# Scan layer with its front and tail in another order, the gate on the Vector engine, a semaphore per first weight and three unread products

## What is computed

```
x = x + 0.5 * _L0_ffn_ref(_layernorm(x), ...)     # mixture of experts
x = x + _L0_attn_ref(_layernorm(x), ...)          # windowed attention
x = x + 0.5 * _L0_ffn_ref(_layernorm(x), ...)     # mixture of experts
x = x + 0.5 * _L1_ffn_ref(_layernorm(x), ...)     # ternary feed-forward
x = x + _L1_attn_ref(_layernorm(x), ...)          # scan layer
x = x + 0.5 * _L1_ffn_ref(_layernorm(x), ...)     # ternary feed-forward
```

```
delta = softplus(delta @ dt_proj_w.T + dt_proj_b)
h = exp(delta * a) * h + delta * b * u            # per token, channel and state
y = sum over the states of h * c
y = (y + u * D_param) * silu(res)
return y @ out_proj_w.T + out_proj_b
```

## Time and profile before

| | us |
|---|---|
| median of 3 runs | 563.32 |
| lowest and highest of them | 561.24, 566.46 |
| profiled execution, its own time | 567.4 |
| its span, first to last instruction | 565.7 |

### The profile page before, as it was taken

How to read it: one execution, slowest core, us unless ns; L and a number is a source line. 1 busy time by engine, 2 the same in 40 slices (tenths; PEclk the granted TensorE clock), 3 DMA queues, 4 the chain that set the end, 5 groups by cost and what they waited for, 6 DMA issues and landing times.

```text
span 565.7 us, 10087 instructions
## 1 busy us (share of the span) xinstructions
PE 478.8 (85%) x3866; PEld 293.2 (52%) x3866; DVE 441.8 (78%) x884; ACT 269.4 (48%) x417; POOL 311.8 (55%) x232
## 2 busy tenths in 40 slices
PE   3999988999999999999588689787688778687995
PEld 2676777787776767776232234233233323245664
DVE  4578778676769566667965999999899989998753
ACT  1426665555556523656784637343343334320742
POOL 3158301202100011567301998999999999994574
PEclk9999999989899889999985798989989979999998
DMA  7000000000000000000019544354553345100011
GB/s 214 2 0 2 5 1 2 3 2 3 2 2 3 2 0 2 2 0 2 0 28 390 232 206 156 122 223 159 213 222 148 149 166 224 56 2 0 2 37 38
DMA packets 12322, 42.74 MB, mean 76 GB/s; under 512 B 2857, under 2 KB 8754, under 8 KB 10226
## 3 DMA queue, kind: packets, MB, share of 16 engines
q1 hardware_dynamic: 11458, 41.56, 19.2%
q10 hardware_dynamic: 816, 0.53, 0.3%
HBM read 40.78 MB, written 1.31 MB: 74 GB/s over the span
## 4 chain that ended last, share of the span: by engine, by line
PE 41%; DVE 22%; issue 16%; POOL 12%; ACT 6%; DMA 1%; POOLq 0%; ACTq 0%; DVEq 0%
DVE hst L1030 7%; PE bk L441 6%; PE bk L447 6%; PE bk L704 5%; PE bk L690 5%; POOL hC L1101 4%; PE bk L677 3%; DVE xnT L278 3%; PE bk L1172 3%; POOL dBu L1084 3%; DVE dBu L1009 2%; PE bk L665 2%; ACT g L836 2%; PE bk L1120 2%; POOL powers L292 2%
## 5 line engine op out<-in xcount | busy, mean ns | idle before, releaser
L1101 POOL TENSOR_TENSOR hC<-hst,rows 128x1024 f32<-128x1024 f32 x63 | 147.2, 2382 | 3.6 <-DVE hst L1030 3.6
L1030 DVE TENSOR_TENSOR_SCAN hst<-bk,dBu 128x1024 f32<-128x1024 f32 x64 | 144.3, 2275 | 4.5 <-POOL dBu L1084 4.5
L1172 PE MATMUL bk<-hC,ident 128*128 128x512 f32 x256 | 126.7, 629 | 2.8 <-ACT ysb L1251 1.6
L1261 ACT ACTIVATE bk<-delta,aneg 128x1024 f32<-128x1024 f32 x64 | 71.5, 1118 | 108.2 <-DVE hst L1030 108.0
L285 POOL TENSOR_TENSOR veps<-mv,lneps 128x4 f32<-128x4 f32 x24 | 5.7, 239 | 165.4 <-DVE mv L257 165.3
L1172 PEld LDWEIGHTS bk<-hC,ident 128*128 128x128 f32 x256 | 50.7, 201 | 55.9 <-issue 45.0
L514 ACT ACTIVATE rows<-bk 128x512 f32<-128x512 f32 x64 | 38.1, 597 | 63.9 <-PE bk L441 63.9
L1152 PE MATMUL bk<-s,sel 96*128 96x512 bf16 x96 | 32.4, 422 | 38.2 <-DVE dBu L1009 38.1
L560 DVE TENSOR_REDUCE smax<-bk 128x4 f32<-128x512 f32 x64 | 43.6, 682 | 24.6 <-PE bk L677 24.6
L1009 DVE TENSOR_TENSOR dBu<-bk,du 128x1024 f32<-128x1024 f32 x48 | 57.6, 1201 | 6.3 <-PE bk L1152 5.3
L836 ACT COPY g<-bk 128x512 f32<-128x512 f32 x64 | 37.4, 584 | 48.5 <-PE bk L690 47.9
(11 more groups left out here) (172 smaller groups left out, 757.6 us busy)
## 6 DMA issues: line engine op xcount, KB each, us to landing
rows<-c_rows SPq DMA_DIRECT2D x16, 2048.0 KB, 7.1
rows<-c_rows SPq DMA_DIRECT2D x4, 1024.0 KB, 9.6
x<-in_x_dram SPq DMA_DIRECT2D x4, 256.0 KB, 5.0
out_dram<-x SPq DMA_DIRECT2D x4, 256.0 KB, 2.3
wmoe<-in_w_dram ACTq DMA_DIRECT2D x2, 256.0 KB, 5.6
wup<-in_upT_dram SPq DMA_DIRECT2D x1, 256.0 KB
wdn<-in_downT_dram SPq DMA_DIRECT2D x1, 256.0 KB
wproj<-in_in_wT_dram SPq DMA_DIRECT2D x1, 256.0 KB
```

The costliest lines, as they stand in the source:

```text
L1030: nc.vector.tensor_tensor_scan(hst[k % 3][:, :], dA[k % 2][:, :], dBu[k % 3][:, :], 0.0, ALU.mult, ALU.add).then_inc(m2["scan"], 1)
L1101: nc.gpsimd.tensor_tensor(hC[k % 4][:, :], hst[k % 3][:, :], crep[:, k % 12, :], ALU.mult).then_inc(m2["hC"], 1)
L1172: last = nc.tensor.matmul(bk01[:, r * CH:(r + 1) * CH], ident[:, :], hC[k % 4][:, r * CH:(r + 1) * CH], start=(k % NS == 0), stop=(k % NS ...
L1261: nc.scalar.activation(dA[k % 2][:, :], delta[:, i, :], ACT.Exp, scale=aneg[:, h * NS + n:h * NS + n + 1]).then_inc(m2["dA"], 1)
```

## The change

Six edits are joined:

1. Each first weight has a semaphore of its own (`w_gate`, `w_up`, `w_down`). PE waits for each just ahead of its first use in chunk 0.
2. PE's queue opens with three products of the identity against itself, repeated to 512 columns. They are written to `bank[0]` to `bank[2]`, and nobody reads them.
3. DVE applies the norm of chunk 3 inside `conv_chunk(1)`, between taps 2 and 3. `x_proj(0, 0)` moves behind `in_proj(3)`. ACT's copy `take_xdbc(0)` moves ahead of the silu of chunk 2.
4. `take_sum` on ACT and `gate` on POOL are gone. DVE gates units 0 to 2 straight from PSUM (`gate_sum`, after step 3 of the next unit), and PE's first sum of the next unit waits for this.
5. `hC` of the last two steps is made by DVE, one more than before.
6. Both output biases are added by POOL ahead of the scan, once the last convolution is done.

```diff
@@ PE, first use of the weights, and the head of its queue
+                    if f is moe0 and c == 0:
+                        pe.wait_ge(w_gate, 16)
...
+                if f is moe0 and c == 0:
+                    pe.wait_ge(w_up, 16)
...
+                if f is moe0 and c == 0:
+                    pe.wait_ge(w_down, 16)
...
-            pe.wait_ge(w_moe, 16 * len(first_loads))
             pe.wait_ge(set_pool, 1)
+            for r in range(3):
+                nc.tensor.matmul(bank[r % 4][:, :].rearrange("p (a k) -> p a k", a=TPC), ident[:, :],
+                                 ident[:, :].rearrange("p (o k) -> p o k", o=1).to_broadcast([P, TPC, P]),
+                                 start=True, stop=True)
@@ front: conv_chunk, ssm1_vector, ssm1_tensor, ssm1_scalar, ssm2_tensor
+                if norm and k == DC - 2:
+                    n_m1.second(dve, norm)
...
-            conv_chunk(dve, 1, 1)
-            n_m1.second(dve, 3)
+            conv_chunk(dve, 1, 1, norm=3)
...
-                if c + 2 == NC:
-                    x_proj(pe, 0, 0)
...
+                if c == NC - 1:
+                    take_xdbc(act, 0)
...
+            x_proj(pe, 0, 0)
             x_proj(pe, 0, 1)
@@ scan: DVE's gate, the last two products
+            def gate_sum(i):
+                b, h = UNITS[i]
+                dve.wait_ge(m2["sum"], NS * (i + 1))
+                if i == 0:
+                    dve.wait_ge(m1["g"], NC * HV)
+                nc.vector.tensor_tensor(g[:, h, b * L:(b + 1) * L], bk01[:, :], g[:, h, b * L:(b + 1) * L], ALU.mult
+                                        ).then_inc(m2["yg"], 1)
...
+                if i > 0 and n == 3:
+                    gate_sum(i - 1)
...
+            for k in range(STEPS - 2, STEPS):
+                dve.wait_ge(c_rep[k // 4 % 3], 16 * (k // 12 + 1))
+                dve.wait_ge(m2["sum"], k - 3)
+                nc.vector.tensor_tensor(hC[k % 4][:, :], hst[k % 3][:, :], crep[:, k % 12, :], ALU.mult
+                                        ).then_inc(m2["hClast"], 1)
@@ POOL
+            pool.wait_ge(m1["conv"], NC)
+            for b in range(B):
+                out_bias(b)
             for k in range(STEPS):
...
-                if i > 0 and n == 6:
-                    gate(i - 1)
@@ PE, add_state
-                    pe.wait_ge(m2["y"], k // NS)
+                    pe.wait_ge(m2["yg"], k // NS)
@@ ACT
-                if i > 0 and n == 4:
-                    take_sum(i - 1)
```

More of the change, by code:

```diff
@@ L161, in macaron_kernel @@
         x_inp = [sem(f"x_inp{c}") for c in range(NC)]
-        w_moe = sem("w_moe")
+        w_gate, w_up, w_down = sem("w_gate"), sem("w_up"), sem("w_down")
         set_pool = sem("set_pool")
@@ L218, in macaron_kernel @@
         m2 = {k: sem("m2_" + k) for k in (
-            "xp", "xdbc", "hi", "rest", "mid", "s3", "dt", "delta", "zc", "du0", "du", "B", "dBu", "dBup", "dA", "scan", "hC", "sum", "y", "yg", "op", "xupd", "bias", "hClast")}
+            "xp", "xdbc", "hi", "rest", "mid", "s3", "dt", "delta", "zc", "du0", "du", "B", "dBu", "dBup", "dA", "scan", "hC", "sum", "yg", "op", "xupd", "bias", "hClast")}
         c_out = [sem(f"c_out{b}") for b in range(B)]
@@ L889, in macaron_kernel, with conv_chunk @@
         xp_of = [bk67, bk01]
-        def conv_chunk(dve, c, r):
+        def conv_chunk(dve, c, r, norm=None):
             link = stepper(dve, m1["cstep"], c * (DC - 2))
@@ L979, in take_u, with take_xdbc @@
             i.then_inc(m1["u"], 1)
+        def take_xdbc(act, b):
+            act.wait_ge(m2["xp"], b + 1)
+            act.wait_ge(set_xdbc, 1)
+            nc.scalar.copy(xdbc[b][0:KS3 + RK, :], xp_of[b][0:KS3 + RK, :]).then_inc(m2["xdbc"], 1)
         def ssm1_scalar(act):
@@ L1031, in ssm2_vector @@
                                              ALU.mult, ALU.add).then_inc(m2["scan"], 1)
-            last_k = STEPS - 1
+                if i > 0 and n == 3:
+                    gate_sum(i - 1)
             dve.wait_ge(m2["scan"], STEPS)
-            dve.wait_ge(c_rep[last_k // 4 % 3], 16 * (last_k // 12 + 1))
-            dve.wait_ge(m2["sum"], last_k - 3)
-            nc.vector.tensor_tensor(hC[last_k % 4][:, :], hst[last_k % 3][:, :], crep[:, last_k % 12, :], ALU.mult
-                                    ).then_inc(m2["hClast"], 1)
+            for k in range(STEPS - 2, STEPS):
[3 more added lines that the diff above has]
+                                        ).then_inc(m2["hClast"], 1)
             def out_add(b):
@@ L1045, in ssm2_vector @@
             n_ter1.first(dve, 0)
-            dve.wait_ge(m2["sum"], STEPS)
-            last_b, last_h = UNITS[-1]
-            nc.vector.tensor_tensor(g[:, last_h, last_b * L:(last_b + 1) * L], bk01[:, :],
-                                    g[:, last_h, last_b * L:(last_b + 1) * L], ALU.mult).then_inc(m2["yg"], 1)
+            gate_sum(len(UNITS) - 1)
             n_ter1.second(dve, 0)
@@ L1067, in delta_u @@
                                         ).then_inc(m2["du"], 1)
-            def gate(i):
-                b, h = UNITS[i]
-                pool.wait_ge(m2["y"], i + 1)
-                nc.gpsimd.tensor_tensor(g[:, h, b * L:(b + 1) * L], ysb[:, :], g[:, h, b * L:(b + 1) * L], ALU.mult
-                                        ).then_inc(m2["yg"], 1)
             def spread_times_du(k):
@@ L1090, in ssm2_pool @@
                     spread_times_du(k + 2)
-                if k == 0:
-                    pool.wait_ge(m2["dBu"], 2)
-                    out_bias(0)
-                if k == STEPS - 1:
-                    out_bias(1)
+                if k == STEPS - 2:
                     break
@@ L1162, in add_state @@
             def add_state(k):
-                if k == STEPS - 1:
-                    pe.wait_ge(m2["hClast"], 1)
+                if k >= STEPS - 2:
+                    pe.wait_ge(m2["hClast"], k - STEPS + 3)
                 else:
@@ L1214, in ssm2_scalar @@
         def ssm2_scalar(act):
-            def take_xdbc(b):
-                act.wait_ge(m2["xp"], b + 1)
-                act.wait_ge(set_xdbc, 1)
-                nc.scalar.copy(xdbc[b][0:KS3 + RK, :], xp_of[b][0:KS3 + RK, :]).then_inc(m2["xdbc"], 1)
             def take_hi(b):
@@ L1242, in softplus @@
                 nc.scalar.activation(delta[:, i, :], z[:, :], ACT.Softplus).then_inc(m2["delta"], 1)
-            def take_sum(i):
-                act.wait_ge(m2["sum"], NS * (i + 1))
-                if i > 0:
-                    act.wait_ge(m2["yg"], i)
-                else:
-                    act.wait_ge(m2["dt"], HV)
-                    act.wait_ge(c_out[0], 16)
-                nc.scalar.copy(ysb[:, :], bk01[:, :]).then_inc(m2["y"], 1)
             def decay(k):
@@ L1275, in ssm2_scalar @@
                 if k == 1:
-                    take_xdbc(1)
+                    take_xdbc(act, 1)
                 if k == 2:
@@ L1319, in scan_weights @@
             last.then_inc(set_dve, 1)
-        first_loads = [
-            (wg[:, :], Wg), (w1s[:, :], w1), (w2s[:, :, :], w2.rearrange("(k p) n -> p k n", p=P)),
-        ]
         loads = [
@@ L1463, in _ @@
         def _(act):
-            for dst, src in first_loads:
-                act.dma_start(dst, src).then_inc(w_moe, 16)
+            act.dma_start(wg[:, :], Wg).then_inc(w_gate, 16)
+            act.dma_start(w1s[:, :], w1).then_inc(w_up, 16)
+            act.dma_start(w2s[:, :, :], w2.rearrange("(k p) n -> p k n", p=P)).then_inc(w_down, 16)
             act.preload_act_table(ACT.Exp)
```

1 line of the change is left out of this document (removed).

## The result

| | before | after |
|---|---|---|
| median (runs) | 565.35 us (20) | 560.96 us (20) |
| lowest to highest | 560.64 to 572.16 | 558.55 to 564.57 |
| ratio, 95% interval | | 0.993 (0.9905 to 0.9954) |
| profiled execution, its span | 567.4, 565.7 | 558.55, 556.8 |

The change gains 4.4 us (0.8% between the medians; by the interval 2.6 to 5.4 us). Forecast were 7.1 us and 556.2 us, with a range that ends at 560.5. The base moved too: over 20 runs the kernel before stands at 565.35, not at the 563.32 of three runs, so of the 4.8 us by which 556.2 is off, 2.0 are the base and 2.7 the change.

What follows compares the result with a forecast made beforehand. No single engine bounds the whole span: PE at the start, POOL in the scan units. Terms -4.0 - 1.3 - 1.4 + 0.9 - 1.3 = -7.1 us, from 563.32 to 556.2; range 552.0 to 560.5.

Steps and rivals of the forecast that it cites:

- Start, -4.0: Start of the kernel: PE's transposes begin near 8.0 instead of 9.07 and the clock rises early; 4.0 us gained.
- the rival of no early clock: Start: the unread products do not raise the clock early, start only -1.05, sum -4.1, 559.2 us; chance 0.10.
- the 1.05 for the semaphores: Start: PE's transposes wait for DVE's first norm instead of all three first weights; 1.05 us gained.
- Front, -1.3: Scan layer before the scan: norm of chunk 3 earlier, `x_proj(0, 0)` off the path to `in_proj(3)`; 1.3 us gained.
- the rival of the better front: Front: clock stays high, `dt_proj(1)` and `x_proj(1, 0)` take half, -3.2 us more, 553.0 us; chance 0.12.
- Units, -1.4: Scan units, scan(15) to scan(63): POOL loses a gate per unit, DVE gains one and becomes the bound; 1.4 us gained.
- the new wait: Unit starts: PE's first sum waits for DVE's gate, delaying the spread; +0.9 us over three units, bounds 0 to 4.5.
- the rival of the costly wait: Unit starts: PE at 1.2 GHz each time, new wait +4.5 instead of +0.9, sum -3.5, 559.8 us; chance 0.14.
- Blocked gate: Units: POOL blocks DVE's gate as it did the last `hC`, 4.45 us per gate, 13.4 in all, 569.6 us; chance 0.04.
- Tail, -1.3: End of the scan: DVE's two last `hC` run without POOL's bias, the last gate waits for PE; 1.3 us gained.
- The next layer follows rigidly: After the last gate: the next layer simply shifts with it, with no gain beyond the tail's 1.3 us.

Runs made afterwards that it cites:

- repeated spreads: Changed kernel with PE's last spread before its wait for DVE's gate made six times instead of once in units 1 to 3; 559.62 us, ratio 0.9881.

## Why the prediction was wrong

Point by point, by its own steps:

- **Start, -4.0: right.** 4.26 in the profile, each part as worked out: PE 1.27 earlier, the logits 1.06, the up blocks 3.54. What the forecast took as certain holds in five profiles of seven: when the clock falls again, 1.8 to 3.6 us are lost. One profile in seven ends where the rival of no early clock, given 0.10, would have ended, though by a rise and a fall. And the 1.05 for the semaphores is a gain only with the products; alone they gave 0.2.
- **Front, -1.3: too small, measured -2.8.** The norm is 1.3 earlier as said. The missed half is the step that held `in_proj(3)` at the low clock to 285.7. The low stretches moved with the work, and the four blocks took 3.70 us, not 4.9; `dt_proj` stayed slow, so this is not the rival of the better front. Where `in_proj(3)` did meet the low clock, with the gate one step earlier, `dt_proj` got the time back: the forecast had counted the low clock at both.
- **Units, -1.4 with +0.9 for the new wait: together -0.5, measured +3.2.** This is the step that failed, and the term that was mis-sized is the new wait. DVE waited 1.46 + 1.42 + 1.18 = 4.1 us behind the three gates, near the top of the 0 to 4.5 that I had worked out. The -1.4 was of the right sign but too large: the changed kernel without the 4.1 us of waits would be 0.9 under the kernel before, and with the gate one step earlier it was -0.5 and -1.2 (149.64 and 148.85 against 150.09). I had discounted the wait because "it takes a low clock in all three units". For the old queue that was right: in the eight profiles with ACT's copy the first sum of a unit was slow (2.99 to 3.65 us) in unit 1 of seven and took 1.95 or 1.96 in the other 17 units. But with the gate on DVE and no repeated spreads, in four profiles, PE stood for 2.45 to 3.84 us ahead of that place in every unit, and the first sum was slow (2.70 to 3.75 us) in 12 of 12; with PE kept at work there it was fast in two of three. So the low clock comes with the longer pause, which the change itself brings, and I had priced it as chance. A row already pointed there, since the kernel before ran this sum at the low clock with PE waiting only 0.52 ahead of it. This was the rival of the costly wait, given 0.14. That its sum of -3.5 is close to the -4.4 measured is in part luck: it had this stretch right (+3.1), and its misses elsewhere were the forecast's.
- **Blocked gate: refuted.** The three gates in the units run at 1.20 us while POOL makes `hC`; at the fourth POOL is nearly idle. The Trainium skill, SBUF — State Buffer, section "Who interferes with whom", says that a Vector instruction with at most one SBUF input, outside the two-port modes, does not contend with GpSimd. The gate has one such input, and the trace agrees, in three of three.
- **Tail, -1.3: too small, measured -2.5.** The last gate is as forecast (10.41 to 9.15), down to the 0.4 taken off because scan(63) comes earlier against PE's queue: without edit 4 the gate comes at 8.6. "The next layer follows rigidly" was wrong: before, POOL's part of the norm stood behind the gate, since DVE's late product had put off the addition to `x` and the statistics; now it is done before the gate, and 1.25 us more go.
- **Sum.** With the start at its average: -3.4 - 2.8 + 3.2 - 2.5 = -5.5, beside -4.4 measured (2.6 to 5.4). What makes the 1.1 that is left is open. The mean granted clock does not tell: over the 20 runs it was 0.932, with edit 4 undone 0.940, but the units already account for that. From scan(15) to scan(63) the changed kernel's profile has 27.3 us at 0.50 and the other 13.7, and 13.6 x 0.5 / 557 = 0.012.

So two misses on the good side (1.5 in the front, 1.2 in the tail) paid for part of the one on the bad side (3.7 in the units).

## What to carry to other kernels

Before an operation moves to another engine, look up who waits for its result and where that engine's queue puts it: one position in DVE's queue was worth 3.6 to 4.4 us here, and the whole move, with what it costs in the tail, between -0.1 and 0.6. Price a wait of PE with the work behind it at 1.2 GHz, wherever the trace shows the low clock at that place even once, and above all where the change makes PE's wait longer. And cut the traces at the same instructions: three stretches that repeated within 0.1 us in most profiles carried the verdicts, while whole spans and the untouched part wandered by 6 us.
